# Lookup tables kept in SBUF: ten whole tables in five pairs, one for half of the samples, and a new order of the last steps

## The reference

```python
e = jnp.stack([tbl_0[ids[:, 0]], ..., tbl_25[ids[:, 25]]], axis=1)        # 512 x 26 x 128
combined = jnp.concatenate([dense_features[:, None, :], e], axis=1)       # 512 x 27 x 128
interactions = jnp.einsum('bfd,bgd->bfg', combined, combined)
z = jnp.concatenate([dense_features, interactions[:, iu, ju]], axis=1)    # iu < ju
h = jnp.concatenate([z, r_dense_features], axis=1)
h = jnp.maximum(h @ W_top1 + b_top1, 0.0)                                 # 607 -> 512
h = jnp.maximum(h @ W_top2 + b_top2, 0.0)                                 # 512 -> 256
y = h @ W_top3
```

## Time and profile before

| what | us |
|---|---|
| median of 3 runs | 138.47 (138.45 to 138.56) |
| the profiled execution's own time | 138.15 |
| its span, first to last instruction | 136.6 |
| PE busy with matmuls | 108.7 (80%) |
| VectorE busy | 76.6 (56%) |
| ScalarE busy | 62.5 (46%) |
| POOL busy | 63.5 (46%) |
| mean granted TensorE clock | 0.874 |

### The profile page before, as it was taken

The page is one execution under the profiler, slowest core; times in us unless marked ns, Lnnn a source line. Parts: engine busy times, 40 slices in busy tenths (PEclk is TensorE's granted clock), DMA queues, the critical chain, the costliest instruction groups (busy, mean ns, idle before and its releaser), DMA issues.

```text
span 136.6 us, 2523 instructions
## 1 busy us (share of the span) xinstructions
PE 108.7 (80%) x927; PEld 86.5 (63%) x927; DVE 76.6 (56%) x181; ACT 62.5 (46%) x168; POOL 63.5 (46%) x70
## 2 busy tenths in 40 slices
PE   5984999629447049999999932797799999999992
PEld 2462788427122037788888731696699998898880
DVE  4679998063220089999996020176591906787401
ACT  3669640250000498967552030166565537558220
POOL 8778788787786277847567785007000000000000
PEclk9999599995955555999999995559999999999999
DMA  4899979996121019942222221001100000000000
GB/s 100 283 345 351 325 218 307 350 330 202 42 61 44 14 43 308 286 156 67 70 70 74 73 58 47 11 5 35 28 0 24 1 6 21 2 5 0 0 0 1
DMA packets 8972, 14.90 MB, mean 109 GB/s; under 512 B 2340, under 2 KB 3904, under 8 KB 8832
## 3 DMA queue, kind: packets, MB, share of 16 engines
q1 hardware_dynamic: 6896, 10.68, 24.0%
q0 software_dynamic: 1920, 3.94, 10.2%
q10 hardware_dynamic: 144, 0.13, 0.3%
HBM read 14.47 MB, written 0.00 MB: 106 GB/s over the span
## 4 chain that ended last, share of the span: by engine, by line
PE 67%; another core or an unknown queue 13%; issue 9%; ACT 5%; DMA 3%; DVE 1%; SPq 1%; ACTq 0%; DVEq 0%
PE gram_ps L694 16%; PE gram_ps L696 15%; PE gram_ps L639 14%; PE layer_ps L647 8%; PE turn_ps L606 6%; PE layer_ps L668 6%; DMA table_sb<-in_hot_tables 3%; ACT table_hi L398 1%; ACT layer_ps L404 1%; PE turn_ps L647 1%; ACT hidden_t L456 1%; ACT pairs L443 1%; PE gram_ps L647 1%; DVE one_hot L519 1%
## 5 line engine op out<-in xcount | busy, mean ns | idle before, releaser
L372 POOL DMA_INDIRECT rows<-in_gathered_tables,row_at x60 | 60.6, 1010 | 31.9 <-issue 16.9
L694 PE MATMUL gram_ps<-one_hot,table_hi 128*128 128x512 f32 x94 | 42.7, 454 | 12.8 <-issue 7.1
L696 PE MATMUL gram_ps<-one_hot,table_lo 128*128 128x512 f32 x94 | 41.4, 440 | 1.2 <-issue 0.9
L519 DVE TENSOR_SCALAR one_hot<-hot_ids_sb,row_ids 128x1024 fp32r<-128x1024 int16 (+1 forms) x52 | 34.8, 702 | 5.2 <-remote 2.7
L694 PEld LDWEIGHTS gram_ps<-one_hot,table_hi 128*128 128x128 f32 x94 | 20.1, 214 | 21.9 <-issue 11.0
L548 DVE COPY pairs<-gram_ps 27x128 f32<-27x128 f32 (+3 forms) x76 | 19.7, 259 | 20.6 <-PE gram_ps L639 19.7
L639 PE MATMUL gram_ps<-features_t 128*59 128x54 f32 x512 | 20.5, 236 | 7.5 <-issue 7.3
L508 DVE TENSOR_TENSOR table_lo<-table_sb,layer_ps 128x512 fp32r<-128x512 f32 (+1 forms) x25 | 16.1, 646 | 17.4 <-ACT layer_ps L404 10.9
L639 PEld LDWEIGHTS gram_ps<-features_t 128*59 128x59 f32 x512 | 18.3, 150 | 10.2 <-issue 9.7
L696 PEld LDWEIGHTS gram_ps<-one_hot,table_lo 128*128 128x128 f32 x94 | 20.3, 216 | 6.4 <-issue 2.6
L443 ACT COPY pairs<-gram_ps 27x128 f32<-27x128 f32 (+3 forms) x68 | 15.9, 233 | 15.1 <-PE gram_ps L639 14.4
(11 more groups left out here) (42 smaller groups left out, 29.8 us busy)
## 6 DMA issues: line engine op xcount, KB each, us to landing
table_sb<-in_hot_tables SPq DMA_DIRECT2D x22, 256.0 KB
hot_ids_sb<-in_hot_ids SPq DMA_DIRECT2D x5, 256.0 KB
w_pairs_sb<-in_w_pairs SPq DMA_DIRECT2D x1, 1024.0 KB
rows<-in_gathered_tables,row_at POOLq DMA_INDIRECT x60, 2.6
w_dense_sb<-in_w_dense SPq DMA_DIRECT2D x1, 512.0 KB
w_sb<-in_w SPq DMA_DIRECT2D x1, 512.0 KB
table_sb<-in_hot_tables SPq DMA_DIRECT2D x3, 128.0 KB, 2.2
dense_sb<-in_dense_f SPq DMA_DIRECT2D x1, 256.0 KB
```

The lines of the kernel that those rows point to most:

```text
L372: pool.indirect_dma_start(rows[:, p % rows_ring, m, :], None, gathered_tables, bass.IndirectOffsetOnAxis(ap=row_at[:, t, at:at + 1], axis= ...
L519: nc.vector.tensor_scalar(one_hot_at(g, c)[:, 0:size, :], hot_ids_sb[:, g % ids_ring, 0:size, :], row_id(g, c), None, ALU.is_equal).then_i ...
L694: nc.tensor.matmul(hot_bank(g, t), piece_columns(table_hi, q, c), one_hot_at(g, c)[:, t, :], start=(c == 0), stop=False)
L696: last = nc.tensor.matmul(hot_bank(g, t), piece_columns(table_lo, q, c), one_hot_at(g, c)[:, t, :], start=False, stop=(c == GROUP_PARTS[g] ...
```

## The change

- Table 0 moves from the first group to the last, and only samples 256 to 511 (`LATE`) are looked up by one-hot: 20 matmuls of 256 columns. For samples 0 to 255 it is gathered: passes 0 and 5 have four gathers instead of three and four transposes, 62 gathers in all. The first group is now a pair.
- The first group's pieces are of 2, 2 and 4 parts. For its first four pieces (`DIRECT`) VectorE takes the high part from SBUF, and ScalarE makes no PSUM copy.
- `TURN_BEHIND`, `LOW_BEHIND` and ScalarE's order of splits and copies follow the new groups.
- The first gather takes its row numbers from the ids as they are; half of the zeroing of `pairs` moves from POOL to VectorE.
- `place_hot(5)` copies one bank, by ScalarE alone; the wait for `last_placed` is gone.
- Behind the hot stage, turns, products and layers change places on PE, ScalarE and VectorE.

```diff
-HOT_GROUPS = ((0,), (2, 3), (1, 7), (13, 16), (19, 21), (23, 25))
-GROUP_PARTS = (10, 10, 8, 8, 8, 8)
+HOT_GROUPS = ((1, 7), (2, 3), (13, 16), (19, 21), (23, 25), (0,))
+GROUP_PARTS = (8, 10, 8, 8, 8, 10)
+LATE = 256
...
-        return ((0, 2), (2, 4), (6, 4))
+        return ((0, 2), (2, 2), (4, 4))
...
-TURN_BEHIND = {(1, 4): 0, (1, 9): 1, (2, 3): 2, (2, 7): 3, (3, 3): 4, (3, 7): 5, (4, 3): 6, (4, 7): 7, (5, 3): 8, (5, 7): 9}
...
+TURN_BEHIND = {(1, 1): 0, (1, 5): 1, (1, 9): 2, (2, 3): 3, (2, 7): 4, (3, 3): 5, (3, 7): 6, (4, 3): 7, (4, 7): 8, (5, 9): 9}
...
+DIRECT = 4
...
+        def early(p):
+            return p // PASSES * P < LATE
+
         def gathers_of(p):
 
-            return SINGLE if p % PASSES == 0 else GROUPS
+            return SINGLE + early(p) if p % PASSES == 0 else GROUPS
...
-                nc.gpsimd.memset(pairs[:, :, 1, :, :], 0.0).then_inc(pairs_zeroed, 1)
+                nc.gpsimd.memset(pairs[:, 1, 1, :, :], 0.0).then_inc(pairs_zeroed, 1)
...
-                        if q >= 2:
+                        if q < DIRECT:
+                            continue
+                        if q >= DIRECT + 2:
...
-                split(pieces_of(1)[0:2])
+                split(pieces_of(1)[0:1])
+                split(pieces_of(1)[1:2])
                 split(pieces_of(1)[2:4])
                 place_hot(0)
+                place_pass(turn_in[1, 1])
                 split(pieces_of(1)[4:])
                 split(pieces_of(2)[:2])
-                place_pass(turn_in[1, 4])
+                place_pass(turn_in[1, 5])
                 split(pieces_of(2)[2:])
                 place_pass(turn_in[1, 9])
                 split(pieces_of(3)[:2])
...
+                    if q < DIRECT:
+                        dve.wait_ge(hi_made, q + 1)
+                        high = piece_columns(table_hi, q).bitcast(F32)
...
-                nc.vector.tensor_tensor(piece_columns(table_lo, q), piece_columns(table_sb, q),
-                                            hi_banks[q % 2][:, 0:PIECES_HOT[q][3] * dim], ALU.subtract).then_inc(lo_made, 1)
...
+                    nc.vector.tensor_tensor(piece_columns(table_lo, q), piece_columns(table_sb, q), high, ALU.subtract).then_inc(lo_made, 1)
...
-                dve.wait_ge(part_used, len(PARTS))
-                for first, end in ((0, BLOCK), (BLOCK, batch)):
-                    nc.vector.tensor_copy(features_t[:, first // 2:end // 2, n_hot, :],
...
                 pairs_of_dve(6)
+                fold(6)
                 pairs_of_dve(7)
-                fold(6)
                 fold(7)
...
                 turn_pass(PASSES * 2)
+                products(2)
                 turn_pass(pass_of(8))
-                products(2)
+                products(3)
                 turn_pass(pass_of(9))
-                products(3)
...
                 products(5)
+                layer2(1)
                 turn_pass(pass_of(12))
+                layer1(2, (0, 1))
                 turn_pass(pass_of(13))
-                layer2(1)
+                layer1(2, (2,))
                 products(6)
+                layer1(2, (3,))
                 turn_pass(pass_of(14))
-                layer1(2, (0,))
                 products(7)
-                layer1(2, (1, 2))
                 turn_last_pass()
-                layer1(2, (3,))
                 products(8)
```

More of the change, by code:

```diff
@@ L354, in _ @@
                 nc.gpsimd.memset(ident[:, :], 0.0).then_inc(ident_zeroed, 1)
-                for kind, parts in enumerate((GROUP_PARTS[-1], max(GROUP_PARTS))):
+                for kind, parts in enumerate((min(GROUP_PARTS), max(GROUP_PARTS))):
                     nc.gpsimd.iota(row_ids[:, kind, 0:parts], pattern=[[1, parts]], base=0, channel_multiplier=parts,
@@ L409, in place_hot @@
                     act.wait_ge(part_used, parts_through(g, GROUP_PARTS[g] - 1))
[L410 to L413, removed]
+                    first = first_sample(g)
+                    for t in range(len(HOT_GROUPS[g])):
+                        act.copy(features_t[:, first // 2:batch // 2, 1 + hot_table(g, t), :],
+                                 hot_bank(g, t)[:, first:batch].rearrange("p (b two) -> p b two", two=2)).then_inc(hot_placed, 1)
                 turn_in = {place: p for place, p in TURN_BEHIND.items()}
@@ L426, in _ @@
                 split(pieces_of(3)[:2])
-                for g in range(2, n_groups):
-                    place_hot(g - 1)
-                    if g + 1 < n_groups:
-                        split(pieces_of(g + 1)[2:])
-                    if (g, 3) in turn_in:
-                        place_pass(turn_in[g, 3])
-                    if g + 2 < n_groups:
-                        split(pieces_of(g + 2)[:2])
-                    if g == n_groups - 1:
-                        place_hot(g)
-                    place_pass(turn_in[g, 7])
+                place_hot(1)
+                split(pieces_of(3)[2:])
+                place_pass(turn_in[2, 3])
+                split(pieces_of(4)[:2])
+                place_pass(turn_in[2, 7])
+                place_hot(2)
+                split(pieces_of(4)[2:])
+                place_pass(turn_in[3, 3])
+                split(pieces_of(5)[:2])
+                place_pass(turn_in[3, 7])
+                place_hot(3)
+                split(pieces_of(5)[2:])
+                place_pass(turn_in[4, 3])
+                place_pass(turn_in[4, 7])
+                place_hot(4)
+                place_hot(5)
+                place_pass(turn_in[5, 9])
                 def pairs_of_act(n, quadrants=(0, 1)):
@@ L491, in _ @@
                 nc.vector.memset(ones[:, :], 1.0).then_inc(ones_made, 1)
+                nc.vector.memset(pairs[:, 0, 1, :, :], 0.0).then_inc(pairs_zeroed, 1)
                 dve.wait_ge(first_ids_in, 16)
@@ L529, in _ @@
                         one_hot_part(g, c)
-                        if (g, c) in LOW_BEHIND:
-                            low_part(LOW_BEHIND.index((g, c)))
+                        for q, place in enumerate(LOW_BEHIND):
+                            if place == (g, c):
+                                low_part(q)
                         if (g, c) == (1, 8):
@@ L537, in _ @@
                 nc.vector.tensor_copy(features_t[:, :, 0, :], dense_sb[:, :].rearrange("p (b two) -> p b two", two=2)).then_inc(dense_placed, 1)
-                dve.wait_ge(part_used, len(PARTS))
-                for first, end in ((0, BLOCK), (BLOCK, batch)):
-                    nc.vector.tensor_copy(features_t[:, first // 2:end // 2, n_hot, :],
-                                          hot_bank(n_groups - 1, 1)[:, first:end].rearrange("p (b two) -> p b two", two=2)).then_inc(last_placed, 1)
                 def pairs_of_dve(n):
@@ L776 @@
     ids = _np.asarray(inputs["ids"])[order]
-    single = ids[:, list(GATHERED[:SINGLE])].reshape(-1, 128, SINGLE).transpose(1, 0, 2)
+    looked_up_late = HOT[-1:]
+    singles = looked_up_late + GATHERED[:SINGLE]
+    single = ids[:, list(singles)].reshape(-1, 128, 1 + SINGLE).transpose(1, 0, 2)
     by_unit = ids[:, list(GATHERED[SINGLE:])].reshape(-1, UNITS_PER_TILE, UNIT, GROUPS, TOGETHER)
     by_unit = by_unit.transpose(4, 2, 0, 1, 3).reshape(128, -1, UNITS_PER_TILE * GROUPS)
-    starts = _np.cumsum([0] + [tables[i].shape[0] for i in GATHERED])[:-1].astype(_np.int32)
-    single_starts = _np.tile(starts[None, :SINGLE], (128, 1))
-    unit_starts = _np.tile(_np.repeat(starts[SINGLE:].reshape(GROUPS, TOGETHER).T, UNIT, axis=0), UNITS_PER_TILE)
+    in_memory = looked_up_late + GATHERED
+    starts = _np.cumsum([0] + [tables[i].shape[0] for i in in_memory])[:-1].astype(_np.int32)
+    single_starts = _np.tile(starts[None, :1 + SINGLE], (128, 1))
+    unit_starts = _np.tile(_np.repeat(starts[1 + SINGLE:].reshape(GROUPS, TOGETHER).T, UNIT, axis=0), UNITS_PER_TILE)
     table_starts = _np.concatenate([single_starts, unit_starts], axis=1).astype(_np.int32)
```

78 lines of the change are left out of this document (50 added, 28 removed).

## The result

The changed kernel takes 145.49 us, the median of four runs (143.78, 144.31, 146.67, 147.15); the kernel before, run beside it, takes 138.51 (138.45 to 139.08). The ratio is 1.0392, with a 95% interval of 1.0328 to 1.0455: slower. The profiled execution took 143.78 us for a span of 142.0, where before it was 138.15 for 136.6, so the traces have 5.4 us to explain. Two of the changed kernel's four executions fell in a slower state; the ratio takes the other two alone, 143.78 and 144.31, and fits those 5.4 us, while the medians stand 7.0 us apart.

What follows compares the result with a forecast made beforehand. Bound by a PE stop of some 20 us, blamed on POOL's unbroken gathers, then a PE-bound stage and tail. Terms -2.3 + 0.2 + 2.2 + 4.0 - 0.3 = +3.8 on 138.47 gave 142.3 us; 8-in-10 range 133.5 to 148.5.

Steps and rivals of the forecast that it cites:

- the likeliest case: The forecast itself: POOL's longer first run delays PE; 142.3 us, own range 140 to 145, chance 0.40.
- the terms ahead of the tail: Before the tail: halved matmuls -2.3, extra transposes +0.2, longer POOL run +2.2, pass 10 joining it +4.0 us.
- While POOL gathers without a pause, PE's signals come late and PE at last stops; a pause of POOL lets them through.: Rule inferred from coincidence in two places, the hot stage's stop and its end; the delay passes on one for one.
- Pass 10 joins the run, +4.0: POOL's first run: pass 1 is turned in time, so three more gathers follow without a pause; +4.0 us, bounds 0 and 8.0.
- POOL's first run longer, +2.2: Passes 0 and 5 have four gathers, lengthening POOL's first run and delaying the signal: +2.2 us, bounds 0 and 2.7.
- The rival with the split run: POOL pauses near 25 us waiting for VectorE's rows, letting signals through sooner: 134 us, 131 to 137, chance 0.27.
- Half-width matmuls, -2.3: Last group of the hot stage: 20 table matmuls go from 512 to 256 columns; -2.3 us, bounds -2.3 and 0.
- Group 0, no gain: Start: 32 matmuls out by 13 us instead of 20, but PE meets the same stop; 0, bounds -3 and 0.
- The four low parts, no price: First pieces: VectorE low parts reading two SBUF operands cost nothing; the skill's rule would add 1 to 2 us.
- The end of the hot stage, 0: Gap before products(0), up to 1.7 us, may go, but POOL's run then holds PE: 0, bound -1.7.
- The tail, -0.3: After the hot stage, reordering turns, products and layers wins idle PE time: -0.3 us, bounds -1.1 and +0.6.

Runs made afterwards that it cites:

- the rows found early: Changed kernel with find_other_rows behind one-hot (1,0) instead of (1,8), so POOL does not pause after its 16th gather: 144.88 us, ratio 1.0405.
- the kernel with two memsets: Changed kernel with two POOL memsets of 1024 columns after the gathers of each odd pass: 135.55 us, ratio 0.9865.
- the trace without breaks: Kernel before with the change's tail order on PE and ScalarE, VectorE in its old order, on the other chip: 107.76 us, ratio 1.0306.

## Why the prediction was right or wrong

The side came out, and the size within the range (142.3 us forecast, 145.5 measured, just outside the 140 to 145 of the likeliest case), but by luck: the terms ahead of the tail gave +4.1 us where the trace has +2.1, and the tail gave -0.3 where it has +3.3.

- **"While POOL gathers without a pause, PE's signals come late and PE at last stops; a pause of POOL lets them through."** The first half is shown on the first chip by five kernels: breaks in the gathers, idle or not, took the stop away in both kernels (128 to 156 records in the stretch that held 55 and 69, a few of them products where the hot stage ended sooner). The second half is too narrow: a pause is not needed, since signals also came within a run, 3 to 6 us late in the changed kernel and 15 us late with the rows found early. And it is no rule of the kernel, as I had it: on the other chip the same gathers hold nothing.
- **"Pass 10 joins the run, +4.0", "POOL's first run longer, +2.2".** Failed as put. The rival with the split run happened, for the reason it gave (finding the rows early took the pause away), and gave no gain, where it had 134 us: the second run took in passes 9 to 11 and the stop came back. PE did not turn pass 1 sooner either (24.86 against 24.57 before), since it had stood from 20.0 to 22.99. Through products(2) it cost 2.1 us, where my terms without the tail gave +4.1. Undoing the split changed nothing that could be measured, so the step that failed is the rule itself, that a pause shifts the time one for one. The length of the run does not price the stop. How often a break comes seems to matter (0.9575 with short breaks after every pass, 0.9865 with long ones after every second), but what sets the length of a stop was not found.
- **Half-width matmuls, -2.3.** Right for one matmul, but no gain of that size is seen. At the end of the hot stage they stand 0.12 us apart; from 77.2 to 80.0 us, at a granted clock of 0.50 (1.2 GHz, the lower of its two levels), they stand 0.21 to 0.22 apart, as a matmul of 512 columns does at full clock, and such a one stands 0.43 apart at the lower (24.01, 24.43 in PE's timeline). With the hold at their start, the 20 took 5.6 us, from 75.07 to 80.63, where 20 of full width at 0.23 would take 4.6 (PE's timeline):

```profile
79.59 0.41 PE L737 MATMUL gram_ps<-one_hot,table_lo 128*128 128x256 f32 x1
79.80 0.40 PE L735 MATMUL gram_ps<-one_hot,table_hi 128*128 128x256 f32 x1
...
80.39 0.28 PE L735 MATMUL gram_ps<-one_hot,table_hi 128*128 128x256 f32 x1
80.51 0.28 PE L737 MATMUL gram_ps<-one_hot,table_lo 128*128 128x256 f32 x1
```

- **Group 0, no gain.** Right, and for the reason given: seven matmuls ahead at 13.3 us, four behind at 26.
- **The four low parts, no price.** Nearly. They took 0.37 us each, and the two gathers beside them, at 5.12 and 6.42, took 1.00 and 1.03 us, where the kernel before has 0.95 and 0.94: 0.14 us on POOL. The 1 to 2 us that the Trainium skill's rule allowed ("SBUF — State Buffer", section "SBUF: two separate sides") did not come.
- **The end of the hot stage, 0.** Right: products(0) begins at once, at 81.05, and is then held until 85.86.
- **The tail, -0.3 (bounds -1.1 and +0.6).** Wrong, measured +3.3 in the trace, 1.0277 and 1.0306 by runs. I summed the idle time to be won and the copies that lose their cover, and never asked what stands behind the moved blocks: products(6) waits behind layer-1 blocks that wait for fold(5). That is the term outside its bounds, and it is most of the loss: 3.3 of the 5.4 us.

Left open: whether the changed kernel is slower than the one before on a chip that does not hold PE. It was not run there. The tail costs 3% on both chips, and the halved table and the fuller POOL are not priced there.

## What to carry to other kernels

Before work is moved ahead on an in-order engine, look up what the moved piece waits for, and what that could run at once now stands behind it. A stop that no dependency in the code explains may belong to the chip: run the same kernel on a second one before a schedule is built around it. Kernels with memsets between POOL's gathers took 1 to 4% less time than the kernel before on one chip, and others with such memsets 7 to 15% more than it on the other.

## What the hardware showed unexpectedly

- Two chips of one kind differ by a quarter on the same program (138 and 104.6 us). On the slow one PE's signals are held while POOL issues indirect gathers, and then PE itself: it moves in steps of about 0.7 us and goes on 0.8 to 2.8 us after the gathers end, or within the run after a stop of up to 15 us. The granted clock falls with the stop (0.62 from 42.0 to 58.4 us); on the other chip it is 1.00 in the trace without breaks. What holds PE, and in what the two chips differ, was not found. Every time given here is of an execution that was also recorded, so no run shows if the hold is there without the recording.
- While POOL set memory, VectorE's one-hot parts stretched. In the kernel with two memsets, VectorE's timeline has two of them beside the memset from 23.43 to 25.85 us:

```profile
23.95 2.45 DVE L571 TENSOR_SCALAR one_hot<-hot_ids_sb,row_ids 128x1024 fp32r<-128x1024 int16 x2
```

Two take 1.41 us beside gathers. The two memsets took 2.42 us, where the pair at 65.05 took 1.98. The Trainium skill ("SBUF — State Buffer", section "SBUF: two separate sides") has a port pair that VectorE and GpSimd lock in turn; the trace agrees for a memset, and far less for a gather, beside which the one-hot parts kept their 1.41 us.
